# Attention's row maxima from the four leading part products, two heads at a time in two row tiles of TensorE

## The reference, cut to what matters

```
h = layernorm(x) * (1 + ca) + sa                      # sa, ca, ga from the conditioning, per sequence
q = split_heads(h)                                    # queries are h itself
k = split_heads((h @ w_dk + b_dk) @ w_uk + b_uk)
v = split_heads((h @ w_dv + b_dv) @ w_uv + b_uv)
q, k = rope(q), rope(k)
attn = softmax(einsum('bhid,bhjd->bhij', q, k) / sqrt(8))
x = x + ga * (einsum('bhij,bhjd->bhid', attn, v) merged over heads @ w_o + b_o)
```

## Time and profile before

| | |
|---|---|
| median of three runs | 3188.53 us |
| the profiled execution, its own time | 3185.01 us |
| its span in the trace | 3183.2 us |
| mean granted TensorE clock | 0.934 |
| attention stage (row maxima) | about 51 to 617 us of the span |
| TensorE, VectorE, ScalarE, GpSimd busy, whole span | 86%, 79%, 70%, 71% |

### The profile page before, as it was taken

One profiled execution on the slowest core, in us unless ns is written; L12 is line 12 of the kernel. 1 busy time (PEld: TensorE's weight loads), 2 busy tenths in 40 slices (PEclk: granted clock), 3 DMA queues, 4 the chain that ended last, 5 costly groups with the idle time before them and its releaser, 6 DMA issues. The chain is left out here.

```text
span 3183.2 us, 56565 instructions
## 1 busy us (share of the span) xinstructions
PE 2733.4 (86%) x18747; PEld 2079.7 (65%) x18747; DVE 2515.7 (79%) x3550; ACT 2236.9 (70%) x4091; POOL 2259.3 (71%) x1731
## 2 busy tenths in 40 slices
PE   5999999829999977888888989888998888779984
PEld 3555555418999834666666666666766666679983
DVE  5788888723444446999999999999999999967993
ACT  2677777612222249999999999999999998656651
POOL 3356667552333348999999999999999999733664
PEclk6999999959999988999999999999999999889995
DMA  6555656316666662222222222222222222322231
GB/s 140 106 107 117 117 113 119 78 47 194 197 190 195 164 218 81 81 75 71 85 80 82 82 74 79 81 81 84 75 72 86 80 82 80 93 56 82 74 87 39
DMA packets 209174, 321.85 MB, mean 101 GB/s; under 512 B 37786, under 2 KB 118070, under 8 KB 204282
## 3 DMA queue, kind: packets, MB, share of 16 engines
q1 hardware_dynamic: 195666, 299.13, 34.9%
q0 software_dynamic: 12224, 18.42, 1.9%
q10 hardware_dynamic: 1008, 0.72, 0.1%
HBM read 269.92 MB, written 55.84 MB: 102 GB/s over the span
## 5 line engine op out<-in xcount | busy, mean ns | idle before, releaser
L1824 POOL TENSOR_TENSOR resid_x<-s_ux,s_B_rows 128x1024 f32<-128x1024 f32 x256 | 605.3, 2365 | 83.7 <-PE s_y L2554 82.7
L2385 DVE TENSOR_TENSOR_SCAN resid_x<-s_dA,resid_x 128x1024 f32<-128x1024 f32 x256 | 582.3, 2275 | 28.8 <-ACT s_dA L2036 23.2
L2393 DVE TENSOR_TENSOR_SCAN resid_x<-s_late,s_back_in 128x1024 f32<-128x1024 f32 x256 | 583.9, 2281 | 20.2 <-ACT s_late L2046 17.1
L2554 PE MATMUL s_y<-identity,resid_x 128*128 128x128 f32 x4096 | 558.7, 282 | 9.6 <-issue 8.8
L2554 PEld LDWEIGHTS s_y<-identity,resid_x 128*128 128x128 f32 x4096 | 498.6, 146 | 65.1 <-issue 40.6
L1832 POOL TENSOR_TENSOR resid_x<-resid_x,s_C_rows 128x1024 f32<-128x1024 f32 x192 | 454.0, 2365 | 0.9 <-DVE resid_x L2385 0.9
L798 DVE TENSOR_REDUCE a_row_max<-a_maxscores 128x2 f32<-128x512 f32 x512 | 337.5, 683 | 67.9 <-PE a_maxscores L1012 62.3
L2400 DVE TENSOR_TENSOR resid_x<-resid_x,s_C 128x1024 f32<-128x1024 f32 x320 | 382.7, 1196 | 6.0 <-PE s_C L2529 6.0
L2541 PE MATMUL s_back_in<-identity,resid_x 128*128 128x128 f32 x2048 | 292.3, 289 | 98.9 <-ACT resid_x L2057 52.6
L2036 ACT ACTIVATE s_dA<-s_dt,s_A 128x510 f32<-128x510 f32 x512 | 330.0, 676 | 66.2 <-DVE resid_x L2385 65.1
L2046 ACT ACTIVATE s_late<-s_dt,s_A 128x510 f32<-128x510 f32 x512 | 338.0, 710 | 0.0
(11 more groups left out here) (461 smaller groups left out, 5696.3 us busy)
## 6 DMA issues: line engine op xcount, KB each, us to landing
s_B_rows<-forward_rows SPq DMA_DIRECT2D x256, 256.0 KB, 3.3
e_w<-L_ffn_w_by_expert SPq DMA_DIRECT2D x71, 768.0 KB, 4.5
s_C_rows<-forward_rows SPq DMA_DIRECT2D x192, 256.0 KB, 3.3
a_Q<-split_qk SPq DMA_DIRECT2D x96, 192.0 KB
split_qk<-a_parts SPq DMA_DIRECT2D x32, 384.0 KB
e_x<-slot_inputs SPq DMA_DIRECT2D x71, 132.0 KB
a_K<-split_qk SPq DMA_DIRECT2D x64, 128.0 KB
s_late<-choice_outputs SPq DMA_DIRECT2D x16, 512.0 KB, 5.0
```

Source lines behind the costliest of these rows:

```text
L1824: tt(R[s, 0], ux[par][:], brow[s % BRING][:].unsqueeze(1).broadcast_to([P, C2, W]), ALU.mult).then_inc(S["in_ready"], 1)
L2385: nc.vector.tensor_tensor_scan(r, a, r, 0.0, ALU.mult, ALU.add).then_inc(S["scanned"], 1)
L2393: nc.vector.tensor_tensor_scan(r[:, ::-1], a[:, ::-1], b[:, ::-1], 0.0, ALU.mult, ALU.add).then_inc(S["scanned"], 1)
L2554: last = mm(YP[:, t, c2 * P:(c2 + 1) * P], R[s, d][:, c2, t * P:(t + 1) * P], core.ident[:], is_transpose=True, start=((s, d) == (0, 1) an ...
```

## The change

Three things change. The row maxima are taken from the four leading part products alone (32 rows, `LEAD`) and not from all nine. The rows of `Q9` and `K9` are laid so that rows 0 to 31 are the leading products for the heads 0 to 7 and rows 32 to 63 are the same for the heads 8 to 15; the blocks that are left fill the other rows, all nine are still there for `scores`. And `max_scores` computes head p from rows 0 to 31 and head p+8 from rows 32 to 63, alternating, each into its own bank: two row tiles of the array, 32 rows by 128 columns, at rows 0 and 32. It now waits until both reductions of the pair before are done, and stands once in a slot. The loads become 22, each of 8, 16 or 24 rows of 4 KB, since the two halves of the heads have different row orders.

```diff
+LEAD = 4 * DH
+Q_RUNS = (((0, 0, 2), (2, 0, 2), (4, 0, 3), (7, 2, 1), (8, 2, 1)), ((0, 0, 3), (3, 2, 1), (4, 0, 2), (6, 0, 3)))
+K_RUNS = (((0, 0, 2), (2, 1, 1), (3, 0, 1), (4, 2, 1), (5, 2, 1), (6, 0, 3)), ((0, 2, 1), (1, 2, 1), (2, 0, 2), (4, 0, 2), (6, 1, 1), (7, 0, 1), (8, 2, 1)))
-    LOADS = 3 * PARTS - 1
+    LOADS = sum(len(runs) for runs in (*Q_RUNS, *K_RUNS))
...
-                        for turn in range(PARTS):
-                            first, cut, past = turn * PARTS * DH, (PARTS - turn) * DH, (turn + 1) * PARTS * DH
-                            sp.dma_start(Q9[n][first:past, :, :].rearrange("p h t -> p (h t)"), rows[0]).then_inc(loaded[n], 16)
-                            sp.dma_start(K9[n][first:first + cut, :, :].rearrange("p h t -> p (h t)"), rows[1, turn * DH:]).then_inc(loaded[n], 16)
-                            if turn:
-                                sp.dma_start(K9[n][first + cut:past, :, :].rearrange("p h t -> p (h t)"), rows[1, 0:turn * DH]).then_inc(loaded[n], 16)
+                        for tile, w, runs in ((Q9[n], 0, Q_RUNS), (K9[n], 1, K_RUNS)):
+                            for half in range(2):
+                                for block, part, count in runs[half]:
+                                    sp.dma_start(tile[block * DH:(block + count) * DH, half * PAIRS:(half + 1) * PAIRS, :].rearrange("p h t -> p (h t)"),
+                                                 rows[w, part * DH:(part + count) * DH, half * PAIRS * T:(half + 1) * PAIRS * T]).then_inc(loaded[n], 16)
...
-                        dve.wait_ge(S["max_ps"], H * b + h + 1)
+                        dve.wait_ge(S["max_ps"], PAIRS * b + h // 2 + 1)
...
-                        nc.vector.tensor_reduce(mx[b % 2][:, h, :], MX[:, h % 2], AX.X, ALU.max).then_inc(S["max_done"], 1)
+                        nc.vector.tensor_reduce(mx[b % 2][:, h // 2 + PAIRS * (h % 2), :], MX[:, h % 2], AX.X, ALU.max).then_inc(S["max_done"], 1)
...
-                def max_scores(i, h):
+                def max_scores(i, p):
...
-                        at(pe, S["max_done"], H * b + h - 1)
+                        at(pe, S["max_done"], H * b + 2 * p)
                         for k in range(TC):
-                            last = mm(MX[:, h % 2, k, :], Q9[n][0:KROWS, h, k * P:(k + 1) * P], K9[n][0:KROWS, h, :], start=True, stop=True)
+                            for half in range(2):
+                                lead, h = slice(half * LEAD, (half + 1) * LEAD), p + PAIRS * half
+                                last = mm(MX[:, half, k, :], Q9[n][lead, h, k * P:(k + 1) * P], K9[n][lead, h, :], start=True, stop=True)
...
                 def slot(i, p):
-                    max_scores(i, 2 * p)
+                    max_scores(i, p)
                     scores(i, p)
-                    max_scores(i, 2 * p + 1)
                     values(i, p)
```

More of the change, by code:

```diff
@@ L1007, in max_scores @@
                         n = b % RING
-                        if h == 0:
+                        if p == 0:
                             pe.wait_ge(loaded[n], 16 * LOADS * (b // RING + 1))
-                        at(pe, S["max_done"], H * b + h - 1)
+                        at(pe, S["max_done"], H * b + 2 * p)
                         for k in range(TC):
-                            last = mm(MX[:, h % 2, k, :], Q9[n][0:KROWS, h, k * P:(k + 1) * P], K9[n][0:KROWS, h, :], start=True, stop=True)
+                            for half in range(2):
+                                lead, h = slice(half * LEAD, (half + 1) * LEAD), p + PAIRS * half
+                                last = mm(MX[:, half, k, :], Q9[n][lead, h, k * P:(k + 1) * P], K9[n][lead, h, :], start=True, stop=True)
                         last.then_inc(S["max_ps"], 1)
```

## The result

Four executions after the change took 3257.97 to 3293.83 us, median 3263.57; four before, 3187.10 to 3190.11, median 3188.36. The ratio is 1.024, 95% interval 1.020 to 1.028: slower by 75 us, where 32 us were forecast. The profiled execution took 3257.97 us (span 3256.2), its mean granted clock is 0.918 where it was 0.934. Nearly all of the difference lies in the attention stage.

The account below looks back on a forecast made before the run. TensorE was nearest the bound, VectorE next, tied by waits; TensorE's savings and shape changes came out even, loads cost 0, and the handshake added 32 turns x 1.0 us, giving 3220 us, range 3180 to 3264.

Parts of the forecast that it names:

- Row tiles side by side, changes of shape: TensorE: paired row tiles save 1.76 us a turn, 15 shape changes of 0.12 us add 1.8; comes out even.
- The handshake decides at full clock: Max scores of a pair wait for both reductions of the pair before; slot loop 1.91 us, expected to decide.
- The walk: Slot-by-slot sum of a turn, each slot the longer of TensorE and loop: 18.65 choices, 18.85 weights, 17.6 us early.
- +1.0 us a turn: Net handshake cost in the attention stage: walks differ by 1.2 to 1.35 us a turn, less 0.2 to 0.3.
- the walk of before: Same slot sum for the old order, each reduction waiting for its own scores only: 17.6, 17.5 and 16.3 us.
- the 0.2 to 0.3 us taken off: Deduction per turn because stalls missing in the old order's walk may now lie under the handshake.
- Loads: SyncE's 22 loads issue in 7.3 to 8.6 us; the 16.2 us chain fits under the turn, cost 0.
- Signs: Expected in the trace: turns of 18.5 to 19 us, more max-load waits for reductions, VectorE about 82% busy.
- 32 turns x 1.0 = +32 us: Sum over the attention stage's 32 turns, added to the profiled 3185.0 us to give 3217.
- the range's upper end: Top of the 3180 to 3264 us range, which leaves out part of the two slow rivals above.
- row tiles that don't run side by side: Rival on TensorE: 0.22 us more in nearly every slot, +80 us, 3268 us; chance 0.09.
- loads that land later: Rival on DRAM loads: 5 us later makes the chain 21 us and sets the turn, 3288 us; chance 0.07.

Follow-up runs that it names:

- e3: Changed kernel with one head at a time and two in flight as before: row tiles without the pair, none side by side; 3279.53 us.
- e2: Kernel before with the handshake by pairs alone: 72 rows, old loads, four max scores of a pair one behind the other; 3280.40 us.
- e1: Kernel before with only the 22 loads and new row layout, max scores over 72 rows, one head at a time; 3199.48 us.
- e5: Changed kernel with VectorE's work between the two reductions of a pair moved behind the second; 3318.97 us.
- e6: Changed kernel with scores ahead of max scores in a slot and VectorE's work moved behind a pair's second reduction; 3290.53 us.
- e12: As e11, but the added scores pass reads only the first 32 of 74 rows and stands right behind the max scores; 3321.13 us.
- e11: Changed kernel with scores of slots 3 to 6 computed twice, all 74 rows, same values; 3267.75 us.
- e4: Changed kernel with the scores put ahead of the max scores in each slot; 3240.31 us.

## Why the prediction was right or wrong

**Right, and in size.**
- *Row tiles side by side, changes of shape.* Four max scores in 0.39 us, a hole of 0.10 us at the change, and e3, with the changes but without the pair, within 0.3 us of the turn that 0.12 us a change gives.
- *The handshake decides at full clock.* e2 shows it alone. The walk gave 17.6 us (early), 18.65 (choices) and 18.85 (weights) for the kernel after; the full-clock turns were 17.4, 19.1 and 18.7.
- *+1.0 us a turn.* At full clock it is 18.59 - 17.62 = 0.97 us. In part this is luck: the walk of before gave 17.6 us for the turns with choices, which took 18.2, and the 0.2 to 0.3 us taken off for it were a judgement. By kind the turns grew by 1.0 (early), 0.9 (choices) and 1.1 us (weights), where the walks differ by 1.3, 1.05 and 1.35.
- *Loads.* 22 issues took 8.2 us (7.3 to 8.6 expected), the first sequence waited 10.99 us where it had waited 11.76, and there is no wait in the steady state. e1 puts them, with the new layout, at 7 us, interval 3 to 12. In its trace the excess lies in two turns behind one stall and not in the loads' waits; whether the loads cause that stall is open.
- *Signs.* VectorE 65.13 / 80 = 81% busy at full clock (82% expected), the waits of max scores' loads for reductions up from 50.7 to 78.6 us.

**Wrong: the sum.** "32 turns x 1.0 = +32 us" holds only if every turn runs at 2.4 GHz. The clock of before is 1.00 in the stage; the walks carried it over unsaid to a kernel with more waits and fewer rows at work. That is the step that failed: the granted clock stood in the sum at no cost, without a reason. 12 of the 31 turns were touched by 1.2 GHz and lasted 22.39 us: 42 us net that no term of the sum held, more than the forecast's whole 32. No rival had it either. The time lies just inside the range's upper end (3264 us), and that is luck: the end stood there for row tiles that don't run side by side and for loads that land later, and neither happened.

My expectations of e3, e5 and e6 were wrong after the result was known, though they named the clock: I took it to stay up where holes are short or few in sum, and it made the kernels with the better handshake slower.

**What the change itself did to the clock.** The runs leave two ways, waits (e2: 60 us low from the handshake alone), and 32 rows instead of 72 for the maxima (e3: 157 us low with few waits, but with many changes of shape; e12 against e11 for rows alone, in the scores). From e2 to the kernel after the low time grows from 60 to 115 us, which holds rows and changes of shape together; the part of the rows alone is argued from e12 and e11. How the 115 us split between the two is not settled, nor how much a change of shape adds, which no run varied alone. That e4's clock fell in every second turn, while the total of waits was like that of the kernel after (76.3 us against 78.6), goes with its waits of 1.22 us, but a wait of 1.22 us also passed at 209.7 us without a fall.

## What to carry to other kernels

Before a change that takes work from TensorE or adds waits to it is priced, look at the granted clock of its stage, and give the case "the clock falls" a term of its own: here it cost 42 us net, more than the 30 us by which the turns grew at full clock. Splitting the result into turns at full clock and turns touched by the low one separates the two in a single trace. A busy share near 100% proves neither that the clock will stay nor that the engine is well used (e3: 498 of 500 us busy, 157 us low); and where two banks go to and fro between two engines, handing over both at once takes away the overlap (e2: +2.9%, part of it by the clock).

## What the runs showed of the hardware

- The granted clock depends on how many rows of the array the matmuls and their weight loads use, not on busy time alone: 197 against 37 us at 1.2 GHz for 32 against 74 rows in one pass, at equal times and counts (e12, e11).
- It can fall within 1 us behind a wait of TensorE of 0.88 us (four falls in the kernel after) or 2.89 us (e1), but of 26 waits over 0.8 us in the kernel after only four were followed by one, and the kernel before passed one of 1.01 us without.
- Within the stages, after 100 us, low stretches came in lengths of 6.8 to 68 us; four of the five in the kernel after lasted 20.5 us. Within them TensorE reads 100% busy.
- A change between full shape and row tiles leaves a hole of about 0.10 us in TensorE's stream (367.28 to 367.60 us in the kernel after, less two rounds of 0.11); the one into column tiles was read at 0.12 us from the earlier trace rows.
- The same bytes in pieces of 4 KB a row instead of 8 KB took 0.42 of the DMA engines' time instead of 0.61 at 118 and 117 GB/s (e1_loads). It had no part in the time.
